# Mask row by VectorE, transposed context loaded, one visit for each head group's values, in a new order

## What is computed

```python
# layers 0 and 1: 16 heads of 16, in layer 1 with a fixed mask
scores = jnp.einsum('bhqd,bhkd->bhqk', q, k) / jnp.sqrt(jnp.float32(D_K))
attn = jax.nn.softmax(scores, axis=-1)
out = jnp.einsum('bhqk,bhkd->bhqd', attn, v)
...
# layer 3: one head of 256
scores = jnp.einsum('bqd,bkd->bqk', q, k) / math.sqrt(HEAD_SIZE)
scores = scores + (1.0 - attention_mask)[:, None, :] * -10000.0
probs = jax.nn.softmax(scores, axis=-1)
...
x = x + _L0_xattn_ref(_layernorm(x, axis=-1), ctx_1024, ctx_1024, ...)
x = x + _L0_ffn_ref(_layernorm(x, axis=-1), ...)      # one of 8 experts
x = x + _L1_xattn_ref(_layernorm(x, axis=-1), ctx_1024, ...)
x = x + _L1_ffn_ref(...)                               # three rounds of a small net
x = x + _L2_xattn_ref(...); x = x + _L2_ffn_ref(...)   # linear attention; low-rank experts
x = x + _L3_xattn_ref(..., mask_BxS2_ff1, ...); x = x + _L3_ffn_ref(...)
```

## Time and profile before

| | us |
|---|---|
| three runs | 995.49, 996.83, 1000.37 |
| median | 996.83 |
| the profiled execution's own time | 996.77 |
| its span | 995.0 |
| PE busy | 957.1 (96%) |
| DVE busy | 631.2 (63%) |
| ACT busy | 537.3 (54%) |
| POOL busy | 235.2 (24%) |

### The profile page before, as it was taken

One profiled execution on the slowest core, in us unless ns is written; L12 is line 12 of the kernel. 1 busy time (PEld: TensorE's weight loads), 2 busy tenths in 40 slices (PEclk: granted clock), 3 DMA queues, 4 the chain that ended last, 5 costly groups with the idle time before them and its releaser, 6 DMA issues.

```text
span 995.0 us, 17737 instructions
## 1 busy us (share of the span) xinstructions
PE 957.1 (96%) x6202; PEld 711.6 (72%) x6202; DVE 631.2 (63%) x2222; ACT 537.3 (54%) x1103; POOL 235.2 (24%) x418
## 2 busy tenths in 40 slices
PE   8899889989999999999999999999999999999998
PEld 7665565656587867777587766777687867878777
DVE  4634673577677775767576776875676566736554
ACT  1341646496458643766357743776378444864421
POOL 3104402311340241413231043313131113001200
PEclk9999989999999999999999999999999999999999
DMA  7308823120523121402134023402122004000000
GB/s 249 45 14 235 217 49 70 42 55 2 106 49 64 44 53 33 101 11 49 27 68 77 12 48 71 101 17 67 25 43 59 28 1 91 1 13 1 1 1 22
DMA packets 39927, 56.25 MB, mean 57 GB/s; under 512 B 3968, under 2 KB 35712, under 8 KB 36224
## 3 DMA queue, kind: packets, MB, share of 16 engines
q1 hardware_dynamic: 38448, 46.50, 22.8%
q10 hardware_dynamic: 1392, 8.63, 2.4%
HBM read 39.64 MB, written 13.89 MB: 54 GB/s over the span
## 4 chain that ended last, share of the span: by engine, by line
PE 73%; ACT 9%; DVE 6%; DMA 4%; issue 4%; POOL 2%; SPq 1%; ACTq 0%; DVEq 0%; POOLq 0%
PE bank L1639 10%; PE bank L1966 7%; PE bank L1696 6%; PE bank L1499 6%; PE bank L1718 5%; PE bank L1490 5%; PE bank L1977 4%; PE bank L1611 4%; PE bank L1753 4%; PE bank L1747 3%; PE bank L1699 2%; ACT PT L871 2%; PE bank L1508 2%; ACT QA L858 2%; PE bank L1779 2%
## 5 line engine op out<-in xcount | busy, mean ns | idle before, releaser
L871 ACT ACTIVATE PT<-bank 128x512 f32<-128x512 f32 x256 | 153.2, 598 | 140.2 <-PE bank L1699 78.3
L1639 PE MATMUL bank<-w,xhT 128*128 128x512 f32 x256 | 125.2, 598 | 0.0
L1696 PE MATMUL bank<-QA,KA 104*128 104x256 bf16 x512 | 112.8, 273 | 9.2 <-ACT PT L871 6.7
L1169 DVE CUSTOM_DVE_ANT_0 bank<-bank,maskb 128x256 f32<-128x256 f32 x256 | 101.9, 450 | 23.0 <-PE bank L1611 22.2
L1162 DVE TENSOR_REDUCE mx<-bank 128x2 f32<-128x512 f32 x128 | 84.1, 682 | 32.9 <-PE bank L1611 32.2
L1611 PE MATMUL bank<-KA,QA 96*128 96x256 bf16 x512 | 92.9, 275 | 7.6 <-issue 3.0
L1696 PEld LDWEIGHTS bank<-QA,KA 104*128 104x128 bf16 x512 | 46.7, 99 | 57.0 <-issue 45.7
L1966 PE MATMUL bank<-xhBT,wi 128*128 128x256 f32 x336 | 85.2, 384 | 0.7 <-DVE hT L1473 0.3
L1215 DVE SCALAR_TENSOR_TENSOR x<-bank,one,x 128x256 f32<-128x256 f32 x128 | 61.6, 481 | 34.6 <-PE bank L1639 30.0
L858 ACT COPY QA<-bank 8x256 bf16<-8x256 bf16 (+1 forms) x128 | 67.9, 576 | 16.3 <-PE bank L1677 15.0
L1611 PEld LDWEIGHTS bank<-KA,QA 96*128 96x128 bf16 x512 | 47.3, 100 | 31.3 <-issue 6.7
(11 more groups left out here) (316 smaller groups left out, 2079.8 us busy)
## 6 DMA issues: line engine op xcount, KB each, us to landing
QA<-scratch SPq DMA_DIRECT2D x90, 128.0 KB, 4.4
scratch<-kparts SPq DMA_DIRECT2D x30, 192.0 KB, 2.3
KA<-scratch SPq DMA_DIRECT2D x15, 384.0 KB, 4.6
scratch<-qparts SPq DMA_DIRECT2D x30, 192.0 KB, 2.3
KA<-scratch SPq DMA_DIRECT2D x15, 256.0 KB, 5.5
w<-pack ACTq DMA_DIRECT2D x1, 2409.0 KB, 8.6
wi<-ipack ACTq DMA_DIRECT2D x1, 2304.0 KB, 9.8
xin<-x_in SPq DMA_DIRECT2D x8, 256.0 KB, 5.5
```

The source lines that it names most:

```text
L871: act.activation(PT[:, n % RING, :, :].rearrange("p t s -> p (t s)"), st_bank[:, :], ACT.Exp).then_inc(exp_s, 1)
L1169: last = dve.tensor_tensor_reduce(s, s, maskb[:, t, :], op0=ALU.add, op1=ALU.max, scale=1.0, scalar=-HUGE, accum_out=mx[:, i % 4, n % GH, ...
L1639: last = pe.matmul(bank[n % 2][:, :], xhT[:, kk, t * P:(t + 1) * P], W("exp0", KT)[:, kk, i * 512:(i + 1) * 512], start=(kk == 0), stop=(k ...
L1696: last = pe.matmul(st_bank[:, t * S:(t + 1) * S], KA[m][0:KM, v, t * P:(t + 1) * P], QA[m][0:KM, v, :], start=True, stop=(m == 0))
```

## The change

Five things:

1. The mask row of layer 3 is no longer added by PE. DVE adds it and takes the maximum in one fused instruction for each half of the rows, writing the sum back to the bank.
2. The host passes the context a second time, transposed. SP loads it straight to `ctxT`; the transposes on PE and the copies on ACT go. The loads stand in `next_cin`, ahead of that of `cin`.
3. The values of each group are a visit of their own after its heads (5 heads in, then every 4), with a copy of 128x256 by ACT and one slot of `OT` in place of two. `vaug` has 32 columns for each head in place of 17; `mm` has four slots in place of three.
4. POOL's wait for the use of rstd is a step of its own.
5. All five tables are new. PE has 324 filler products in place of 348.

Counted over the kernel: PE loses 32 transposes, 16 fp32 products of 128x256 and 24 fillers; ACT loses 8 copies of 128x512, has 64 copies of 128x256 to `OT` in place of 32 of 128x512, and 69 table loads in place of 63; DVE has 16 fused instructions in place of 9 reductions; SP has 8 loads of 256 KB more.

```diff
@@ SP @@
+            def turned_ctx(b):
+                sp.dma_start(ctxT[b % CTX][:, :, :].rearrange("p k s -> p (k s)"), ctxT_in[b]).then_inc(ctx_t[b % 2], 16)
             def next_cin(b):
                 if b < B:
-                    sp.wait_ge(ctx_ps, nth(ctx_ps, b - 1, 1))
+                    if b >= CTX:
+                        sp.wait_ge(r3_ps, nth(r3_ps, b - CTX, 1))
+                    elif b == CTX - 1:
+                        sp.wait_ge(qk_ps, 2)
+                    if b >= 2:
+                        sp.wait_ge(ctx_t[b % 2], nth(ctx_t[b % 2], b // 2 - 1, 16))
+                    turned_ctx(b)
                     sp.wait_ge(third_pe, nth(third_pe, b - 1, 2))
...
             sp.dma_start(xin[0][:, :, :], rows(x_in, 0)).then_inc(x_in_s[0], 16)
-            sp.dma_start(cin[:, :, :], rows(ctx_in, 0)).then_inc(c_in_s, 16)
+            turned_ctx(0)
             load(0)
             load(1)
+            sp.dma_start(cin[:, :, :], rows(ctx_in, 0)).then_inc(c_in_s, 16)
@@ ACT @@
             def prepare(b):
-                if b >= CTX:
-                    act.wait_ge(r3_ps, nth(r3_ps, b - CTX, 1))
-                elif b == CTX - 1:
-                    act.wait_ge(qk_ps, 2)
-                evac(ctxT[b % CTX], pb if b else lb, ctx_ps, nth(ctx_ps, b, 1), ctx_t)
-                yield
...
-                        if v >= 9 and (v - 9) % (2 * GH) == 0:
-                            i = q * ITEMS + 2 * ((v - 9) // (2 * GH))
-                            act.wait_ge(pv_ps, i + 2)
+                        if v >= 6 and (v - 6) % GH == 0:
+                            i = q * ITEMS + (v - 6) // GH
+                            act.wait_ge(pv_ps, i + 1)
                             if i:
                                 act.wait_ge(otT_ps, i)
-                            act.copy(OT[:, :, :].rearrange("p g s -> p (g s)"), pv_bank[:, :]).then_inc(ot_s, 1)
+                            act.copy(OT[:, :], pv_bank[:, 0:S]).then_inc(ot_s, 1)
@@ DVE @@
                         dve.wait_ge(L.s["sc_ps"], at(L, "sc_ps", b, 1, h))
-                        link(L.t, dve.tensor_reduce(
-                            L.m2[:, lo:hi], L.bank[h][:, :].rearrange("p (t s) -> p t s", t=T)[:, lo:hi, :], AX.X, ALU.max))
+                        for t in range(lo, hi):
+                            ps = L.bank[h][:, t * S:(t + 1) * S]
+                            last = dve.tensor_tensor_reduce(ps, ps, L.mrow[:, :], op0=ALU.add, op1=ALU.max, scale=1.0,
+                                                            scalar=-HUGE, accum_out=L.m2[:, t:t + 1])
+                        link(L.t, last)
@@ PE @@
             def prepare(b):
-                pe.wait_ge(c_in_s, nth(c_in_s, b, 16))
+                if b == 0:
+                    pe.wait_ge(w_in[0], 16)
...
-                transpose_all(kb, cin).then_inc(ctx_ps, 1)
-                yield
-                pe.wait_ge(ctx_t, nth(ctx_t, b, 1))
+                pe.wait_ge(ctx_t[b % 2], nth(ctx_t[b % 2], b // 2, 16))
                 last = yield from project_T(kb, "wk0", ctxT[b % CTX])
...
-                        if v >= 8 and (v - 8) % (2 * GH) == 0:
...
-                            for g in (2 * pair, 2 * pair + 1):
...
+                        if v >= 5 and (v - 5) % GH == 0:
+                            g = (v - 5) // GH
...
+                            for t in range(T):
+                                for h in range(GH):
+                                    last = pe.matmul(pv_bank[32 * h:32 * h + 32, 0:S], vaug[m][:, t, g * GH + h, :],
                                                      PT[:, (i * GH + h) % RING, t, :], start=(t == 0), stop=(t == T - 1),
                                                      tile_position=(0, 32 * h))
...
                             for kk in range(KT):
-                                pe.matmul(ps, L.xhBT[:, kk, t * P:(t + 1) * P], L.k3[:, kk, :], start=(kk == 0), stop=False)
-                            last = pe.matmul(ps, W("first"), L.mrow[:, :], start=False, stop=True)
+                                last = pe.matmul(ps, L.xhBT[:, kk, t * P:(t + 1) * P], L.k3[:, kk, :],
+                                                 start=(kk == 0), stop=(kk == KT - 1))
@@ TURNS @@
     "tensor":
-        "pwwwpppwwwppwwwwwwwppwwwwwwwwwwwwwwwwwwwwwwwwwwwwwwpwwwwwpwpwwwwwwwwppwwwwwwwwwwwwwsswpsspssvpsvswwvs"
...
+        "pppwwwppwwwwwwwwwwwwwwwwppwwwwpwwwwwwpwpwwwwwwppwwwwwwwwwwwwwwwwwwwwwwwwwwwsswwspspssvsvssvwwvsvspss"
```

More of the change, by code:

```diff
@@ L1 @@
-import itertools
 import numpy as np
@@ L28 @@
 MQ = KM
-VW = HD + 1
 E = 8
@@ L174, in weave, with program @@
             pass
-def program(nc, x_in, ctx_in, mask_in, pack, nomask, ipack, scratch, out):
+def program(nc, x_in, ctx_in, ctxT_in, mask_in, pack, nomask, ipack, scratch, out):
     ctx = ExitStack()
@@ L230, in program @@
         QA = [sb(f"QA{m}", [KM, H, S], BF16) for m in range(2)]
-        vflat = [sb(f"vaug{m}", [P, T, H * VW + 32 - VW]) for m in range(2)]
-        vaug = [v[:, :, 0:H * VW].rearrange("p t (h e) -> p t h e", h=H) for v in vflat]
+        vaug = [sb(f"vaug{m}", [P, T, H, 32]) for m in range(2)]
         kh = sb("kh", [P, T, H])
@@ L349, in program @@
         xh_s = {t: sem(f"xh_{t}", n) for t, n in norms.items()}
-        ctx_ps, ctx_t = sem("ctx_ps", 1), sem("ctx_t", 1)
+        ctx_t = [sem(f"ctx_t{i}", 16) for i in range(2)]
         xh0T_ps, xh0T_s = sem("xh0T_ps", 1), sem("xh0T_s", 1)
@@ L1713, in value @@
                                     pe.wait_ge(attT_s, q)
-                            for g in (2 * pair, 2 * pair + 1):
-                                i = q * ITEMS + g
-                                pe.wait_ge(exp_s, GH * (i + 1))
-                                for t, h in itertools.product(range(T), range(GH)):
-                                    last = pe.matmul(pv_bank[32 * h:32 * h + 32, g % 2 * S:(g % 2 + 1) * S], vflat[m][:, t, (g * GH + h) * VW:(g * GH + h) * VW + 32],
+                            for t in range(T):
+                                for h in range(GH):
+                                    last = pe.matmul(pv_bank[32 * h:32 * h + 32, 0:S], vaug[m][:, t, g * GH + h, :],
                                                      PT[:, (i * GH + h) % RING, t, :], start=(t == 0), stop=(t == T - 1),
                                                      tile_position=(0, 32 * h))
-                                last.then_inc(pv_ps, 1)
+                            last.then_inc(pv_ps, 1)
                             yield
-                        if v >= 10 and (v - 10) % (2 * GH) < 2:
-                            pair, half = (v - 10) // (2 * GH), (v - 10) % (2 * GH)
-                            i = q * ITEMS + 2 * pair + half
-                            pe.wait_ge(ot_s, q * ITEMS // 2 + pair + 1)
-                            pe.wait_ge(negm_s, 2 * (q + 1) * ITEMS)
+                        if v >= 7 and (v - 7) % GH == 0:
+                            g = (v - 7) // GH
+                            i = q * ITEMS + g
+                            pe.wait_ge(ot_s, i + 1)
+                            pe.wait_ge(negm_s, 2 * (q * ITEMS + min(ITEMS, g + 3)))
                             if i:
@@ L1730, in value @@
                             for t in range(T):
-                                last = pe.transpose(ot_bank[:, t * P:(t + 1) * P], OT[:, half, t * P:(t + 1) * P], ident)
+                                last = pe.transpose(ot_bank[:, t * P:(t + 1) * P], OT[:, t * P:(t + 1) * P], ident)
                             last.then_inc(otT_ps, 1)
@@ L2063, in packed @@
         "right": padded(a["L2_ffn_right"].reshape(E * R, D), P, D),
-        "first": padded(np.ones((1, P), np.float32), P, P),
         "wq3t": tiles(a["L3_xattn_Wq"].T), "bq3": column(a["L3_xattn_bq"]),
@@ L2083 @@
         "ctx_in": np.ascontiguousarray(a["ctx_1024"]),
+        "ctxT_in": np.stack([tiles(c.T) for c in a["ctx_1024"]]),
         "mask_in": np.ascontiguousarray(a["mask_BxS2_ff1"]),
```

137 lines of the change are left out of this document (79 added, 58 removed).

## The result

| | before | after |
|---|---|---|
| median of 8 runs | 997.2 us | 1003.5 us |
| lowest, highest | 994.7, 1000.4 | 1001.4, 1007.7 |
| profiled execution, its span | 996.8, 995.0 | 1007.7, 1005.7 |

The changed kernel is slower: the ratio of the times is 1.0067, with a 95% interval of 1.0044 to 1.0091. The forecast was 991.3 us, with a range of 981 to 1002. The profiled execution of the changed kernel (called after from here on) lies 4 us above its median, so its trace overstates the loss.

The account below looks back on a forecast made before the run. PE was taken as full from about 126 to 900 us, latency chains bounding the rest. Behind 126 us -6.9 - 2.2 + 6.4 + 0.9 = -1.8, ahead -2.2 - 1.5 = -3.7; together -5.5 from 996.8: 991.3 us, range 981 to 1002.

Parts of the forecast that it names:

- Part 1: Layer 3's mask row leaves PE: 16 fp32 products of 0.43 us, all behind 126 us, 6.9 us less.
- Part 2: Context loaded transposed, PE's transposes dropped: 2.2 us less in the full stretch and 2.2 at the start.
- the scores of (0,1): First scores of layer 1, batch 0, at 126.31 us before; forecast near 122.6 after a pause of 4 us or more.
- part 4: New order at the wait near 126 us: 0.87 us of PE work moves behind it, counted as +0.9.
- each multiplication taken out or put in counts with its pitch: PE is full from about 126 to about 900 us, so products removed or added there change the time by their pitch.
- DVE's extra time: Two fused mask instructions for one reduction, about 0.3 us more per batch; put at nothing, 2.4 us if uncovered.
- -2.2 in the full stretch: 20 groups of transposes, batches 3 to 7, at 0.44 us for four, between about 126 and 900 us: 2.2 us.
- the dropped filler: The 24 filler products removed by the new order cost nothing if they fall in waits; bound 2.6 us.
- Part 3: Single-group value visits: 29 new ones behind 126 us at 0.22 us, +6.4; first attention gains 1.5 us.
- PE has less to do, and the DMA chain sets the end: At the wait near 126 us the pause lengthens, the start gain of 2.2 + 1.5 stands, 0.87 us not saved.
- one place only (3 us): At the wait near 126 us, a longer pause might stretch the half clock by 6 us, losing 3 us.
- The slower rival: ACT's exponentials in the full stretch hold PE, six more table loads and small copies add 12.6 us: 1003.9; chance 0.18.

Follow-up runs that it names:

- experiment 6: Kernel before, with each layer 3 mask product on PE made twice (16 more fp32 products): 1003.0 us, ratio 1.0051.
- experiment 5: Kernel before with its own tables, only the mask row moved from PE to DVE's fused instruction: 995.7 us, ratio 0.9974.
- experiment 4: Changed kernel with 28 filler products instead of 16 before the first weights: 1002.7 us, ratio 1.0050; start times were also compared over the kept traces.
- experiments 10 and 11: 10: kernel before, each pair visit cut in two, 1009.3 us; 11: changed kernel with early load, 48 of 64 visits cut in two again, 1013.2 us.
- Experiment 1: Changed kernel with the load of the last weights ahead of the copy to mm on ACT's queue: 996.8 us, ratio 0.9990.
- experiment 8: Kernel before with its own tables and pair visits, mask added by DVE and context loaded transposed: 994.9 us, ratio 0.9966.

## Why the prediction was wrong, by its own steps

Two steps failed: the worth of work taken from a full PE (parts 1 and 2), and the date of the scores of (0,1), from which a transfer on ACT's queue had been left out (part 4).

**Part 1, -6.9 us: measured -2.5.** The failing step is "each multiplication taken out or put in counts with its pitch". Putting in nearly does (experiment 6), taking out does not (experiment 5). PE busy in 99% of a stretch did not say that PE sets its length: the ends of products are modelled and overlap the next start (four transposes stand as 0.60 us in the earlier trace rows, and the next work starts after 0.44), so a wait of up to about 0.16 us doesn't show at all, and a chain that ends just when the work does shows nothing either. DVE's extra time I had put at nothing. That fits: the fused form measures 0.449 us, and no wait of PE names it.

**Part 2, -2.2 in the full stretch and -2.2 at the start: measured 0.** For the first it is the same error. At the start I had taken the gain because the transfers chain behind it, and had put the dropped filler at nothing "when they fall in waits". In the two traces PE stays longer at the half pace without it, until about 13 us, before until about 9: the eight records at 12.91 in after still take 1.91 us to the next start, those at 8.70 in the earlier trace rows take 2.03, against 1.77 at the full pace. The weights came later too (7.23 us, where the forecast had 6.5), and the first scores came 1.5 us earlier (35.74 against 37.26), not 2.2. But by the scatter of experiment 4 one pair of traces can't price the start: the means over five traces of each start are 36.2 and 35.1 us. What share of the 2.2 was there stays open.

**Part 3, +6.4 and -1.5.** Both prices are borne out: 0.23 us for a visit instead of 0.22, and where visits were added alone (experiments 10 and 11) the time rose by at least that. That all 6.4 us count in the change itself is not shown, since no run has the new order with pair visits. From the first scores to x the attention takes 68.44 - 35.74 = 32.7 us against 71.78 - 37.26 = 34.5: 1.8 us less. This one doesn't scatter: six traces with the changed kernel's visits and order have 32.7; of nine with the old ones eight have 34.5 or 34.6 and one 35.4. A single visit in after (timeline of PE; the product before it is through at 602.56):

```profile
602.45 0.27 PE L1704 MATMUL bank<-identb,mq 128*104 128x128 bf16 x2
602.65 1.07 PE L1745 MATMUL bank<-PT,vaug 128*32 128x256 f32 x16
603.66 0.28 PE L1723 MATMUL bank<-QA,KA 104*128 104x256 bf16 x1
```

**Part 4, scores of (0,1) at 122.6: measured 129.9.** This is the other miss. The pause of over 4 us came (4.67), but the date was off by 7.3 us. The failing step is "PE has less to do, and the DMA chain sets the end": I had weighed what the new order moves ahead of this wait on PE, and for SP what stands behind the new loads; I had not gone through ACT's queue and asked, for each transfer that it starts, what it now waits for. The load of the last weights came 6.4 us later, took 3.9 us longer, and held PE for 4.84 us. Experiment 1, with the load early, has the scores at 119.9, so the forecast was even too cautious for the rest.

**The clock.** The prediction named it at one place only (3 us). The mean granted clock of the runs is 0.985 for after, 0.989 with the early load, 0.9935 for before. The trace of before, at 0.997, is one of its quieter executions. If time went only with the clock, 0.0083 of 1003 us would be 8.3 us: an upper estimate, since a pause is no longer at half clock. For most of it the clock isn't a cause of its own: of the four stretches, three follow a wait of PE (4.84, 4.67, and 0.96, 0.45 and 1.33 in a row). For the fourth, at 921 us, the trace shows pauses of at most 0.5 us before it. The trace of experiment 1 has the same pauses there (0.45 us and less) and no half clock; against it after falls back by 2.9 us behind that place. No run here settles the cause.

**ACT.** The slower rival gave 1003.9, and 1003.5 was measured, but that is luck: it needed PE's waits for exponentials above 15 us, and they are 8.9. Table loads went to 69 as counted. The one behind which PE paused longest, timeline of ACT in after:

```profile
204.10 1.28 ACT L894 ACT_TABLE_LOAD   x1
205.40 0.60 ACT L894 ACTIVATE PT<-bank 128x512 f32<-128x512 f32 x1
```

The exponential follows at once here too; the drain that the Trainium skill adds ("ScalarE: Activation LUTs", "What ACT_TABLE_LOAD costs") is not in these rows. Yet this load stands ahead of the first exponentials of (1,1), where PE pauses.

**The sum again, with what was measured:** parts 1 and 2 together -3.2 (experiment 8, on the old tables) and the visits +6.4 leave +3.2; the late load adds 6.7: +9.9. Measured is +6.2, so the first attention and the new order otherwise gave back about 3.7 us, of which the first attention has 1.8. The rest of about 2 us is no more than what is left over: the terms come from different kernels, each good to 1 or 2 us. Against the forecast of -5.5, the first error is worth 8.1 us (11.3 less 3.2), the second 6.7.

## What to carry to other kernels

When an order changes, go through each queue that starts transfers and ask of every load what now stands ahead of it, what that waits for, and which other transfers it will then meet; here a load behind a copy of 0.4 us, behind a moved product, cost 6.7 us. Work taken from an engine that is 99% busy is worth its time only if no chain ends at the same place: find the next wait on another engine's result behind it, and see when that result is there. In this kernel adding cost most of what the records say, and removing gave only the slack. And compare several traces before pricing a stretch at the start: one pair said 1.1 us for the filler, a third trace took it back.

## What the runs showed of the hardware that I had not expected

- PE's granted clock differs between runs of one kernel and goes with the time. In the four groups of runs of the kernel before, the median span at a mean clock of 0.997 is 993.0 to 995.2 us, and at 0.993 it is 996.3 to 997.0.
- The start of one and the same code differs between executions by more than the effects looked for there. The eight records of the first projection of the changed kernel took 3.55 us to the next start in one trace and 2.21 in another, after pauses of 2.54 and 2.36 us; with filler until the weights came they took 1.77. The first scores of the unchanged start range over 4.3 us in five traces.
- A load of 2345 KB took 9.4 us to land when issued at 71.3 us and 12.5 when issued at 83.5, among other transfers.
- Cutting 48 visits once more cost 16.4 us without one more product. A visit of products with 32 columns, four side by side in the array, between full-width work costs 0.23 us beyond its products; the rest were waits for exponentials.
